# A recommender kernel whose last stage counts twelve tiles ahead of its gates, and returns its results through TensorE and one store

## The reference

```python
scores = einsum('bhd,bd->bh', hist_emb, user_emb)
user_his_emb = einsum('bh,bhd->bd', scores, hist_emb)
x = concatenate([items_emb, user_his_emb, user_emb], axis=1)   # 2048 x 384
x = dice(batchnorm(x @ W1 + b1, g1, be1), a1)                   # 2048 x 1024
x = dice(batchnorm(x @ W2 + b2, g2, be2), a2)                   # 2048 x 512
return x @ W3 + b3                                              # 2048 x 1
# dice(x, alpha): avg and var over a user's features (var is a SUM of (x-avg)**2 + 0.001)
#   ps = sigmoid((x - avg) / sqrt(var));  ps * x + (1 - ps) * alpha * x
```

## Time and profile before

| | us |
|---|---|
| median of 3 runs | 794.44 (794.24 to 794.94) |
| the profiled execution | 794.12 |
| its span on the core | 792.3 |
| PE busy | 585.3 (74%) |
| DVE busy | 520.2 (66%) |
| ACT busy | 357.9 (45%) |
| POOL busy | 481.9 (61%) |

### The profile page before, as it was taken

The page is one execution under the profiler, slowest core; times in us unless marked ns, Lnnn a source line. Parts: engine busy times, 40 slices in busy tenths (PEclk is TensorE's granted clock), DMA queues, the critical chain, the costliest instruction groups (busy, mean ns, idle before and its releaser), DMA issues.

```text
span 792.3 us, 17056 instructions
## 1 busy us (share of the span) xinstructions
PE 585.3 (74%) x3685; PEld 548.1 (69%) x3685; DVE 520.2 (66%) x1345; ACT 357.9 (45%) x880; POOL 481.9 (61%) x507
## 2 busy tenths in 40 slices
PE   2765678586859576686868878876746899999793
PEld 1664677476858576686868868766635788888683
DVE  8763658384756748476575775774466979974473
ACT  3033345353535344343434544534547857743552
POOL 6377777777777777777777777777711243421025
PEclk9886598787778797877879869788775989999997
DMA  7222222222212122212122222221200000000000
GB/s 228 62 53 51 53 55 55 54 53 51 55 53 55 52 53 54 52 53 54 51 54 55 54 52 53 55 54 52 53 11 0 1 1 1 1 0 1 1 1 0
DMA packets 17606, 34.62 MB, mean 44 GB/s; under 512 B 8472, under 2 KB 8768, under 8 KB 17536
## 3 DMA queue, kind: packets, MB, share of 16 engines
q0 software_dynamic: 14720, 29.14, 14.5%
q1 hardware_dynamic: 2816, 4.66, 1.7%
HBM read 33.76 MB, written 0.01 MB: 43 GB/s over the span
## 4 chain that ended last, share of the span: by engine, by line
issue 29%; PE 28%; DMA 15%; POOL 12%; DVE 9%; ACT 3%; POOLq 1%; DVEq 1%; ACTq 0%; SPq 0%; PEldq 0%
DMA rows<-in_L_rec_user_table_dram,slot_idx 14%; PE ps L1279 13%; POOL rows L465 12%; PE ps L1232 3%; PE ps L1156 2%; PE ps L1339 2%; PE ps L1172 2%; PE ps L1219 2%; DVE prod L736 1%; ACT wide L1123 1%; DVE work L742 1%; PE ps L1334 1%; ACT scaled L1039 1%; DVE stats L729 1%; PE ps L1147 1%
## 5 line engine op out<-in xcount | busy, mean ns | idle before, releaser
L465 POOL DMA_INDIRECT rows<-in_L_rec_user_table_dram,slot_idx x432 | 410.5, 950 | 133.0 <-issue 113.3
L1232 PE MATMUL ps<-ident,scaled 128*128 128x128 f32 x984 | 180.3, 334 | 130.5 <-ACT scaled L1039 130.5
L1039 ACT ACTIVATE scaled<-rows,work 128x128 f32 (+1 forms) x492 | 175.2, 400 | 198.2 <-DVE work L746 149.9
L1232 PEld LDWEIGHTS ps<-ident,scaled 128*128 128x128 f32 x984 | 156.6, 232 | 146.0 <-issue 137.3
L736 DVE TENSOR_TENSOR prod<-rows,ps 128x512 f32<-128x512 f32 x123 | 84.3, 685 | 133.5 <-POOLq L472 116.2
L1279 PE MATMUL ps<-h,w 128*128 128x256 f32 (+1 forms) x576 | 119.4, 369 | 1.2 <-DVE h L867 1.2
L1279 PEld LDWEIGHTS ps<-h,w 128*128 128x128 f32 x576 | 103.2, 200 | 13.1 <-DVE h L867 1.5
L742 DVE TENSOR_REDUCE work<-prod 128x512 f32 (+1 forms) x123 | 84.3, 686 | 22.1 <-DVE prod L736 17.5
L1156 PE MATMUL ps<-wide,h 128*128 128x103 f32 x512 | 77.7, 318 | 0.0
L1156 PEld LDWEIGHTS ps<-wide,h 128*128 128x128 f32 x512 | 76.0, 236 | 0.1
L508 POOL TENSOR_SCALAR work<-work,rest,alphas 128x2048 f32<-128x2048 f32 x7 | 20.1, 2876 | 91.8 <-ACT work L1103 91.8
(11 more groups left out here) (193 smaller groups left out, 757.9 us busy)
## 6 DMA issues: line engine op xcount, KB each, us to landing
rows<-in_L_rec_user_table_dram,slot_idx POOLq DMA_INDIRECT x432, 2.5
w<-in_L_rec_W_dram SPq DMA_DIRECT2D x1, 2048.0 KB, 14.9
w<-in_L_rec_W_dram SPq DMA_DIRECT2D x1, 1536.0 KB, 7.9
h<-in_r_history_users_dram SPq DMA_DIRECT2D x2, 400.0 KB, 3.4
out_dram<-y_col,perm POOLq DMA_INDIRECT x16, 2.1
wide<-in_L_rec_user_table_dram,own_idx POOLq DMA_INDIRECT x5, 5.8
wide<-in_L_rec_item_table_dram,own_idx POOLq DMA_INDIRECT x5, 5.2
last_row<-in_L_rec_user_table_dram SPq DMA_DIRECT2D x1, 64.0 KB, 3.5
```

Of the source, the lines that this page charges most:

```text
L465: nc.gpsimd.indirect_dma_start(rows[:, s, :], None, user_table, bass.IndirectOffsetOnAxis(slot_idx[:, s:s + 1], 0)).then_inc(landed[s], 16)
L1039: nc.scalar.activation(scaled[:, j, :], rows[:, bass.ds((g & (GROUPS - 1)) * GROUP + j, 1), :], ACT.Copy, scale=score[:, bass.ds(g * GROUP ...
L1232: nc.tensor.matmul(pooled_ps, scaled[:, j, :], ident[:, :], start=False, stop=False, skip_group_check=True).then_inc(slot_summed, 1)
```

## The change

- `place_keys` carries four extra columns (104, not 103): the user's partition plus one and the user's tile-column plus one (`WHOSE`), in place of the person number. POOL fills them with two iotas, not one. ACT keeps both in `whose`.
- POOL, in step 4 of the pipeline over the groups, after `normalise(5)`, makes 16 one-hot squares `back` (128x128) and 16 `at_place` (128x16) from `whose`.
- `w3_diag` and its four ACT copies go. The weighted features `zw` are made in SBUF: the first three quarters of users by POOL (12 instructions of 128x512), the last by ACT (4). PE then only transposes `zw` (`turn_weighted`).
- PSUM in the last stage is split 3 (to count), 2 (to gate), 3 (weighted) in place of 4 and 4.
- `EARLY = 12` tiles are counted, and their scale and bias made, before the first gate; the other four are counted between the sums of tiles 0 to 5. Their inverse root is made by DVE alone (`invert_root`: ten dependent instructions on 128x4).
- The sums are spread by POOL (`y_placed`, 128x16), moved to the users' partitions by 16 matmuls with `back` that add up in one PSUM tile, scaled once by DVE, and stored by one plain DMA of SP (64 bytes for each partition).

```diff
--- before.py
+++ after.py
...
-        PERSON, OUT = HIST, HIST + 1
-        ROW = HIST + 3
+        WHOSE, OUT = HIST, HIST + 2
+        ROW = HIST + 4
...
+        zw = h1.rearrange("p m b -> p (m b)")[:, TILES * D2:2 * TILES * D2].rearrange("p (m b) -> p m b", m=M2)
...
+        back = w1.rearrange("p k n -> p (k n)")[:, 4 * CHUNK:4 * CHUNK + TILES * P].rearrange("p (t b) -> p t b", b=P)
...
-        turned_ps = [ps[:, i, :] for i in range(4)]
-        weighted_ps = [ps[:, 4 + i, :] for i in range(4)]
+        counted_ps = [ps[:, i, :] for i in range(3)]
+        turned_ps = [ps[:, 3 + i, :] for i in range(2)]
+        y_ps = ps[:, 0, 0:TILES]
+        weighted_ps = [ps[:, 5 + i, :] for i in range(3)]
...
+            sp.wait_ge(y_kept, 1)
+            sp.dma_start(out.rearrange("(p t) a -> p (t a)", t=TILES), y_out[:, :]).then_inc(stored, 16)
+            sp.wait_ge(stored, 16)
...
-            nc.gpsimd.iota(people[:, :, PERSON], [[1, TILES]], base=0, channel_multiplier=TILES,
+            nc.gpsimd.iota(people[:, :, WHOSE], [[0, TILES]], base=1, channel_multiplier=1,
+                           allow_small_or_imprecise_dtypes=True).then_inc(consts_made, 1)
+            nc.gpsimd.iota(people[:, :, WHOSE + 1], [[1, TILES]], base=1, channel_multiplier=0,
...
+                if i == NARROW + 2:
+                    pool.wait_ge(whose_kept, TILES)
+                    for t in range(TILES):
+                        nc.gpsimd.tensor_scalar(back[:, t, :], col_no[:, :], whose[:, t, 0:1], None, ALU.is_equal).then_inc(backs_made, 1)
+                        nc.gpsimd.tensor_scalar(at_place[:, t, :], col_no[:, 0:TILES], whose[:, t, 1:2], None,
+                                                ALU.is_equal).then_inc(backs_made, 1)
             pipelined(step)
-            pool.wait_ge(perm_kept, TILES)
+            pool.wait_ge(bn_ready[1], 1)
+            for q in range(B // QUARTER - 1):
+                for k in range(M2):
+                    of = slice(q * QUARTER, (q + 1) * QUARTER)
+                    if q == 0 and k < Z_DVE:
+                        pool.wait_ge(z_first, k + 1)
+                    else:
+                        pool.wait_ge(z_normed, M2 * q + k + 1 - Z_DVE)
+                    nc.gpsimd.tensor_scalar(zw[:, k, of], h2[:, k, of], w3c[:, k:k + 1], None, ALU.mult).then_inc(zw_pool, 1)
+            pool.wait_ge(backs_made, 2 * TILES)
             for t in range(TILES):
-                pool.wait_ge(y_kept, t + 1)
-                nc.gpsimd.indirect_dma_start(out, bass.IndirectOffsetOnAxis(perm[:, t:t + 1], 0),
-                                             y_col[:, t:t + 1], None).then_inc(stored, 16)
-            pool.wait_ge(stored, 16 * TILES)
+                pool.wait_ge(y_summed, t + 1)
+                nc.gpsimd.tensor_scalar(y_placed[:, t, :], at_place[:, t, :], y_sum[:, t:t + 1], None, ALU.mult).then_inc(y_moved, 1)
...
-            for t in range(TILES):
-                dve.wait_ge(z_turned, t + 1)
-                nc.vector.bn_stats(stats3[:, t, :], turned_ps[t % 4]).then_inc(z_counted, 1)
-                if t:
-                    dve.wait_ge(z_counted, t)
-                    nc.vector.bn_aggr(mv3[:, t - 1, :], stats3[:, t - 1, :]).then_inc(bn_step[1], 1)
-            dve.wait_ge(z_counted, TILES)
-            nc.vector.bn_aggr(mv3[:, TILES - 1, :], stats3[:, TILES - 1, :]).then_inc(bn_step[1], 1)
-            done = M2 + 3 + TILES
-            dve.wait_ge(bn_step[1], done)
-            nc.vector.tensor_scalar(var2[:, :], mv3[:, :, 1], float(D2), D2 * DICE_EPS, ALU.mult, ALU.add).then_inc(var2_ready, 1)
-            dve.wait_ge(rooted2, 1)
-            nc.vector.reciprocal(inv2[:, :], root2[:, :]).then_inc(inv2_step, 1)
-            dve.wait_ge(inv2_step, 1)
-            nc.vector.scalar_tensor_tensor(minus_arg[:, :], mv3[:, :, 0], -1.0, inv2[:, :], ALU.mult, ALU.mult).then_inc(arg2_ready, 1)
-            def finish(t):
-                dve.wait_ge(y_summed, t + 1)
-                nc.vector.tensor_scalar(y_col[:, t:t + 1], y_sum[:, t:t + 1], rest2[:, 0:1], bias3[:, 0:1],
-                                        ALU.mult, ALU.add).then_inc(y_kept, 1)
-            for t in range(TILES):
+            def count(t):
+                dve.wait_ge(z_for_count, t + 1)
+                nc.vector.bn_stats(stats3[:, t, :], counted_ps[t % 3]).then_inc(z_counted, 1)
+            def aggregate(t):
+                dve.wait_ge(z_counted, t + 1)
+                nc.vector.bn_aggr(mv3[:, t, :], stats3[:, t, :]).then_inc(bn_step[1], 1)
+            def spread(of):
+                dve.wait_ge(bn_step[1], M2 + 3 + of.stop)
+                nc.vector.tensor_scalar(var2[:, of], mv3[:, of, 1], float(D2), D2 * DICE_EPS,
+                                        ALU.mult, ALU.add).then_inc(var2_ready, 1)
+            def make_args(of, before):
+                dve.wait_ge(inv2_step, before)
+                nc.vector.scalar_tensor_tensor(minus_arg[:, of], mv3[:, of, 0], -1.0, inv2[:, of],
+                                               ALU.mult, ALU.mult).then_inc(arg2_ready, 1)
+            def invert_root(of):
+                y, v, x = inv2[:, of], var2[:, of], guess[:, :]
+                dve.wait_ge(var2_ready, 2)
+                nc.vector.tensor_scalar(y.bitcast(I32), v.bitcast(I32), -0.5, float(0x5f3759df), ALU.mult, ALU.add).then_inc(guessed, 1)
+                for i in range(3):
+                    dve.wait_ge(guessed, 3 * i + 1)
+                    nc.vector.tensor_tensor(x, y, y, ALU.mult).then_inc(guessed, 1)
+                    dve.wait_ge(guessed, 3 * i + 2)
+                    nc.vector.scalar_tensor_tensor(x, x, -0.5, v, ALU.mult, ALU.mult).then_inc(guessed, 1)
+                    dve.wait_ge(guessed, 3 * i + 3)
+                    nc.vector.scalar_tensor_tensor(y, x, 1.5, y, ALU.add, ALU.mult).then_inc(guessed if i < 2 else inv2_step, 1)
+            def sum_up(t):
                 dve.wait_ge(gated2, t + 1)
                 dve.wait_ge(z_weighted, t + 1)
-                nc.vector.scalar_tensor_tensor(gate[:, t, :], gate[:, t, :], rest2[:, 1:2], weighted_ps[t % 4],
+                nc.vector.scalar_tensor_tensor(gate[:, t, :], gate[:, t, :], rest2[:, 1:2], weighted_ps[t % 3],
                                                ALU.add, ALU.mult, accum_out=y_sum[:, t:t + 1]).then_inc(y_summed, 1)
+            first, later = slice(0, EARLY), slice(EARLY, TILES)
+            for t in range(EARLY):
+                count(t)
                 if t:
-                    finish(t - 1)
-            finish(TILES - 1)
+                    aggregate(t - 1)
+            aggregate(EARLY - 1)
+            spread(first)
+            count(EARLY)
+            dve.wait_ge(rooted2, 1)
+            nc.vector.reciprocal(inv2[:, first], root2[:, first]).then_inc(inv2_step, 1)
+            make_args(first, 1)
+            aggregate(EARLY)
+            count(EARLY + 1)
+            aggregate(EARLY + 1)
+            sum_up(0)
+            sum_up(1)
+            sum_up(2)
+            count(EARLY + 2)
+            aggregate(EARLY + 2)
+            sum_up(3)
+            sum_up(4)
+            count(EARLY + 3)
+            aggregate(EARLY + 3)
+            spread(later)
+            sum_up(5)
+            invert_root(later)
+            make_args(later, 2)
+            for t in range(6, TILES):
+                sum_up(t)
+            dve.wait_ge(y_home, 1)
+            nc.vector.tensor_scalar(y_out[:, :], y_ps, rest2[:, 0:1], bias3[:, 0:1], ALU.mult, ALU.add).then_inc(y_kept, 1)
...
-                nc.scalar.activation(perm[:, t:t + 1], rows_ps[:, PERSON:PERSON + 1], ACT.Copy).then_inc(perm_kept, 1)
+                nc.scalar.activation(whose[:, t, :], rows_ps[:, WHOSE:WHOSE + 2], ACT.Copy).then_inc(whose_kept, 1)
...
-            for k in range(M2):
-                nc.scalar.activation(w3_diag[:, k, :], ident[:, :], ACT.Copy, scale=w3c[:, k:k + 1]).then_inc(w3_spread, 1)
...
+            last = slice(B - QUARTER, B)
+            act.wait_ge(z_normed, M2 * (B // QUARTER) - Z_DVE)
+            for k in range(M2):
+                nc.scalar.activation(zw[:, k, last], h2[:, k, last], ACT.Copy, scale=w3c[:, k:k + 1]).then_inc(zw_act, 1)
             act.wait_ge(var2_ready, 1)
-            nc.scalar.activation(root2[:, :], var2[:, :], ACT.Sqrt).then_inc(rooted2, 1)
-            act.wait_ge(arg2_ready, 1)
+            nc.scalar.activation(root2[:, 0:EARLY], var2[:, 0:EARLY], ACT.Sqrt).then_inc(rooted2, 1)
             for t in range(TILES):
-                act.wait_ge(z_turned, TILES + t + 1)
-                nc.scalar.activation(gate[:, t, :], turned_ps[t % 4], ACT.Sigmoid, bias=minus_arg[:, t:t + 1],
+                if t == 0 or t == EARLY:
+                    act.wait_ge(arg2_ready, 1 if t == 0 else 2)
+                act.wait_ge(z_turned, t + 1)
+                nc.scalar.activation(gate[:, t, :], turned_ps[t % 2], ACT.Sigmoid, bias=minus_arg[:, t:t + 1],
```

(55 more changed lines are left out.)

37 lines of the change are left out of this document (21 added, 16 removed).

## The result

The changed kernel takes **790.42 us** (median of 5 runs, 788.10 to 791.73) and the kernel before, on the same chip, 794.37 us (794.24 to 794.94): a ratio of **0.9947 [0.9929, 0.9964]**. It is 3.95 us faster. I had forecast 784.6 us, 9.8 us faster, and a range that ended at 787.6 us. The direction was right and the size was not: less than half of the forecast gain is there. The profiled execution took 790.6 us, with a span of 788.8 us.

What follows compares the result with a forecast made beforehand. Behind 744.96 us ACT's normalising, PE's gate pace and POOL's stores and drain bound it. Last sum 3.8 us earlier plus end 6.0 us shorter gives -9.8 us: 784.6 us forecast, own range 783.2 to 786.2, stated range 783.2 to 787.6.

Steps and rivals of the forecast that it cites:

- What bounds the kernel, and the front: Up to 741.7 us gathers, then PE's layer 2; everything moved lies behind 744.96 us; the front changes by nothing.
- The one-hot squares on POOL: 32 compares ahead of group 3's mixing: 7.2 us fits 10.15 us idle; bounds 5 to 17.6 us; loss taken as 0.
- rival 1: PE's clock falls in the new gap behind the counts, slowing gates and perhaps products; 786 to 789 us; chance 0.10.
- The rival that held this mechanism: POOL's compares overrun idle time if one costs above 0.65 us; at 0.7 us each 796.1 us; chance 0.02.
- The weighted features: Behind the second batch norm, POOL's 12 pieces at most 0.7 us each, last at about 752.2 us; hidden.
- The lock: DVE's third normalising instruction may wait for POOL's first weighted piece on shared ports; 0.5 to 0.7 us more; chance 0.25.
- The first gate: Twelve tiles counted early, then bias and 1.28 us table load; first gate at 759.87 us against 762.29, 2.4 us earlier.
- The gates: PE needs 0.88 us per tile, not 1.33; 2.0 us gap at gate 9; last sum 776.80 us, 3.8 us earlier.
- Rivals 1 and 2: Besides rival 1: the second has gates keep 1.33 us per tile with two buffers; 788.4 us; chance 0.08.
- The end: Last sum to span's end 5.7 us, was 11.7; POOL's 4.66 us drain closes it, SP's store 0.4 us behind.

Runs made afterwards that it cites:

- e1: Changed kernel with its 32 POOL compares moved behind the loop over the groups; 1031.34 us, ratio 0.9867 to the kernel before on the same chip.
- e2: Kernel before with only the 32 compares added in step 4, results unused; 1054.78 us, ratio 1.0091 to the kernel before on the same chip.
- e4: Changed kernel with 16 large compares left in step 4, 16 small ones behind the loop; 1031.13 us, ratio 0.9880 to the kernel before.
- e3: e1 with large compares and weightings written as two operations each; 1034.75 us, ratio 0.9901 to the kernel before on the same chip.
- e5: e1 with products of tiles 0 to 5 in PE's gap and weighting as multiply-add; 781.23 us, ratio 0.9847 to the kernel before.
- e6: e1 with the 16 indirect POOL stores of the kernel before, no squares or products; 792.38 us, ratio 0.9978 to the kernel before.

## Why the prediction was wrong

**What bounds the kernel, and the front.** Right. The first batch norm moved by 0.6 us, within what runs differ by (591.4 to 593.9 us in the profiles on chips with quick gathers).

**The one-hot squares on POOL: the step that failed.** The prediction put bounds of 5 and 17.6 us around the 32 compares, wrote "up to 7.5 us over", and then "I take 0". They took 17.2 us. Three things were off. The price: the rows had no compare, and I took one near the iota (which reads nothing) at 0.3 us for the large and 0.15 us for the small; they are 0.59 and 0.31 us, 13.9 us in all. Even my 7.2 us, and the lower end of 5, lay below 32 times my own lower price (0.23 us, 7.4 us). By an estimate from the two sizes (0.28 us more for 112 columns more, 2.5 ns a column) 0.27 of the 0.31 us do not depend on the size. The company: I named DVE's additions as few and let them go; they cost 3.3 us. At 13.9 us undisturbed the overrun would have been 3.8 us; with them it was 7.0, of which 1.9 us were covered (I had 0.7 of slack). And PE's clock: I looked for its fall in the new gap behind the counts (rival 1), where it did not come; it came here, where PE stood idle for 5.51 us, and made the next 16 matmuls 2.5 us longer. 5.1 and 2.5 are the 7.6 us. The rival that held this mechanism counted only from 0.65 us a compare, where it eats the whole gain. The case in between, an overrun that eats half, was in the bounds and in no rival, and so neither in the chances nor in the range, which ended at 787.6 us; with 7.5 us from my own bounds it would have ended at 792. e1, e2 and e4 show it from three sides: compares gone from there, the delay is gone, and the slow matmuls with it; compares alone, both are there; the large half of them, no delay.

**The weighted features.** The size was wrong, 1.56 us and not 0.7, the conclusion right: hidden. POOL was done 19.6 us behind the second batch norm (772.6 us) and not 7.4, which pushed its spreading of the first sums behind 772.5 us, where nobody waited. e3 and e5 made the pieces 0.70 us, and nothing moved. The wait that could have come, PE's on the last pieces, was 1.8 us away.

**The lock.** DVE's three normalising instructions took 1.83 us beside POOL's first piece and 1.46 us before: 0.37 us, where I had drawn 0.5 to 0.7. By the Trainium skill, "SBUF — State Buffer", section "SBUF: two separate sides", a DVE instruction with two inputs in SBUF and a POOL instruction that reads SBUF shut each other out for the whole instruction, and so does a DVE instruction with one input if it runs in a mode that takes both ports. The normalising has one tensor as input; whether it runs in that mode no run here shows, and a wait for a whole instruction is not what the trace shows at this place: DVE's three were done at 755.01 us and POOL's piece only at 755.63 us, and in e5, with a piece of 0.84 us in place of 1.72, DVE's three took 1.84 us all the same. Among the compares it agrees: they read SBUF, DVE's additions there have two inputs, and the small compare that began with a 1.26 us addition at 644.50 us ended 0.12 us behind it. There the rule would have been worth far more. I weighed it at the cheaper of the two places.

**The first gate.** 2.4 us earlier by the prediction, 3.1 us in fact. The part I had wrong is the table load: in the profile before, it waited for PE, and I put it behind the bias. Here it starts at 765.83 us, straight behind the root, while DVE still counts and inverts, and the first gate follows the bias by 0.04 us. 1.3 us won, and 0.6 us lost by counts that came later: 0.2 at the first one, the rest because two more of them than before fell into the time of the lower clock, where they follow each other in 0.85 us and not 0.67.

**The gates.** 16.9 us drawn, 16.9 measured. The gap of PE behind gate 9 was there, 1.67 us for 2.0. Rivals 1 and 2 did not come here: the clock stood at 1.00 from 768.0 us on, and the tiles followed each other in 0.88 us (777.28, 778.18 and 779.06 us are the starts of the weighted turns).

**The end.** Forecast 5.7 us, measured 4.5. The products were 3.49 us for 3.5, the store 1.8 us from its issue to the span's end, where I had 2.0 to its landing and 0.65 behind that. POOL's drain was 3.75 and not 4.66 us; the 4.66 belongs to the kernels with indirect stores at the end (before, e2 and e6), which the change takes away. With it gone the two ways end 0.5 us apart, in the other order.

All stretches but one, then, were within 1.2 us, and their errors sum up to -1.3 us; the one with the term that was set to nothing cost 7.6 (5.1 of waiting and 2.5 of slower matmuls).

## What to carry to other kernels

An operation that an engine has not run in the profile has no price by size: take the upper bound for it, compare this with the idle time that is to hide it, and if the two are close, make the overrun a case of its own with its full cost, not only from the point where it eats everything. Cover is a threshold: it ends where the next engine would have had to wait, not where the idle time ends (here nearly 2 us later). Above it, look at what the wait does to PE's clock, which added 2.5 us to the 5.1 of waiting here. Look for the next idle stretch of the same engine (here 21.8 us, a few lines further down) before squeezing work into the first. And behind the last result, ask which engine's own closing is longest, and let that engine finish first.
